# A two-layer metaformer block on one core: both expert layers with four experts per product, and a new order of work on every engine

## The chip, the core and the metric

The kernel runs on one core of a Trainium2 chip. The metric is the device time of one execution in microseconds (us), and the kernel is compared with itself by the median of several executions. The five engines each work through a list of instructions of their own, in order, and wait for one another on semaphores: TensorE (PE in the profile, with its weight loads as PEld), VectorE (DVE), ScalarE (ACT), GpSimd (POOL) and SyncE (SP, which here issues transfers and follows the control code). TensorE writes to PSUM, eight banks of 512 words in each of 128 partitions; the other three read PSUM or SBUF (GpSimd SBUF alone).

## What is computed

All data is 32-bit floating point. `x` holds 8 images of 32 channels and 24 x 24 points. Four sublayers follow one another, each added to its own input; each normalises first (subtract the mean over the channels, divide by the root of the variance).

```
x = x + conv0(ln_c(x))        # attention of every point to its 3x3 neighbours, 4 heads
t = t + experts(ln_t(t))      # 16 experts, each picks 8 of an image's 576 points
x = x + conv1(ln_c(x))        # products within 9x9 patches
t = t + chain(ln_t(t))        # up to 33 steps, chosen by argmax of one token
```

The second one is where most of the change lies:

```
logits = einsum('bsd,ed->bse', x, gate_w) + gate_b
probs  = softmax(logits, axis=1)                     # over the points
topv, topi = top 8 of probs for each image and expert
pooled = einsum('bked,bke->bed', x[topi], topv)      # 32 numbers per image and expert
h   = gelu(pooled @ weight1[e] + bias1[e])           # 128 hidden units
out = h @ weight2[e] + bias2[e]                      # back to 32
outputs[topi] += topv * out                          # scattered to the picked points
```

With the given data the chain at the end runs one step: a feed-forward layer on all points.

## The kernel before, in words

The images are worked on as two tiles, t = 0 and 1, of four images each: the 128 partitions are 4 images x 32 channels and the 576 points lie along a row, cut into two halves g = 0, 1 of 288. Banks 0 to 3 (`AB`) and 4 to 7 (`CD`) are shared out between the tiles. The order of work is written out by hand, one list per engine; the two tiles are woven into each other so that one tile's products cover the other's waits. Nothing is planned by a program.

A normalisation is `centre` (L451, a product with a centring matrix), squares on ScalarE (`squares`, L867), `variance` (L457, four products onto 32 partitions each), Ln and Exp on ScalarE (`inverse_std`, L881), `widen` (L468, spreads 1/std back over the channels), and `scale` on VectorE (L1049), which multiplies the widened factor in PSUM with the centred input kept in SBUF (`keep`, on ScalarE at L872 in `squares_keep`).

The attention: q, k, v products (L478); VectorE and GpSimd multiply q with nine shifted copies of k (L1067, L391); `head_sum` (L497) adds within a head; the maximum (L1192 to L1197), a subtraction (L1201), Exp (L957), a sum by TensorE into bank 7 (L691 to L694), Ln and Exp of it (L960, L962) and a multiplication (L1205) make the softmax. Then, for u = 0 to 5 (tile u // 3, row of neighbours u % 3), `spread(u)` (L518) gives the weights of a head to its channels: four products that read 32 partitions each, one for each quarter of the points, into banks 4 to 7; `terms(u)` on VectorE (L1074) multiplies the four quarters with v. `spread` waits for each quarter's bank by itself. GpSimd adds the terms up (`gsum`, L410; `x1_raw`, L420), and `add_centred` (L510) lets TensorE add and centre them at once, in banks 0 to 3, for the next normalisation.

The experts, for each tile: `gate` (L530) and the bias (`logits`, L888); `selection` on VectorE (L1086: eight largest, their replacement, and `pick`, L1095, which keeps the eight probabilities), Exp and the inverse sum on ScalarE (`probabilities`, L896); `turn_y`, `turn_pick` and `pooling` (L537, L547, L556) bring points onto partitions and pool the picked ones. `pooled` (L1102) masks the result so that each of the four images keeps its own 32 partitions. `hidden` (L569) is 16 products, one per expert, each with 128 x 128 weights and 4 columns; the weights of an expert lie four times on the partitions. Gelu follows, then `expert_out` (L580), 16 products with 128 x 32 weights and 4 columns, a turn (L588), `expert_blocks` on VectorE (L1110) and `scatter` (L591). For the third normalisation `keep_centred` (L564) first puts the centred input into the bank by two products with the identity, and the scatter adds the centred expert output on top. ScalarE loads another table of functions for Gelu and again for Ln and Exp; between `gelu(0)` and `gelu(1)` it does both (L974 to L981).

The patches (`pixels_out` L603 to `turn_back` L651) and the last normalisation are woven likewise; `choose` (L1147) finds the argmax of one token after the first third of `residual3(0, .)`. GpSimd builds a table of codes that `choose` reads (L401 to L408, on one partition of 627 words) behind its six q x k products. SyncE issues the constants in the order of L330 to L339; `x` of tile 1 and the first constants go through ScalarE's queue.

The lists themselves stand at L666 to L768 (TensorE), L933 to L1003 (ScalarE) and L1173 to L1246 (VectorE). The lines that matter most of them:

```
variance(1, 1); turn_pick(0); widen(1, 1)        # TensorE, L721 to L735
pooling(0); keep_centred(0); gate(1); hidden(0)
turn_y(1); turn_pick(1); expert_out(0)
pooling(1); keep_centred(1); scatter(0)
...
selection(0); turned_pick(0); scale(1, 1); pooled(0); selection(1)   # VectorE, L1213 to L1217
```

Of the kernel before, what the change touches and what calls it, by code (L numbers as in the profile page):

```python
# [9 lines left out]
P = 128  # L10
# [8 lines left out]
ER = E_ * TB  # L19
SC_, NCH = 96, S // 96  # L20
# [18 lines left out]
         ("wb", V2A), ("eb1", H1), ("eb2", C), ("pool", ER), ("own", TB), ("blk", GW), ("ebsel", ER), ("turn", 2 * C),  # L39
# [31 lines left out]
def pack_table(a):  # L71
# [24 lines left out]
    put("gb", np.repeat(a["L0_ffn_gate_b"], TB)[:, None])  # L96
# [7 lines left out]
    put("eb2", a["L0_ffn_weight2"][:, H1, :])  # L104
# [5 lines left out]
    put("turn", np.concatenate([np.eye(C), np.eye(C) - 1 / C], axis=1).astype(np.float32))  # L110
# [14 lines left out]
def expert_table(w):  # L125

    return np.tile(w[:, 0:C, :].transpose(1, 0, 2), (TB, 1, 1)).reshape(P, E_ * H1)
# [21 lines left out]
def metaformer(nc, x, L1_ffn_ffn_w1, L1_ffn_ffn_b1, L1_ffn_ffn_w2, L1_ffn_ffn_b2, L1_ffn_wq, L1_ffn_wk, L1_ffn_wv, L1_ffn_wo,  # L149
# [5 lines left out]
    with ctx:  # L155
# [19 lines left out]
        ew1 = sb("ew1", [P, E_, H1])  # L175
        ew2 = sb("ew2", [P, E_, C])
# [30 lines left out]
        pm = sb("pm", [P, T, ER])  # L207
        hidT = sb("hidT", [H1, T, ER])
        eoutT = sb("eoutT", [C, T, ER])
# [174 lines left out]
        def _(pool):  # L384
# [5 lines left out]

            for t in range(T):  # L391
# [8 lines left out]

            pool.wait_ge(mask_ld, 16 * 2)  # L401
            bits = code[:, :, :].rearrange("p b o -> p (b o)")
            nc.gpsimd.tensor_copy(maskf[:, :], mask_w[:, :]).then_inc(code_st, 1)
            pool.wait_ge(code_st, 1)
            nc.gpsimd.tensor_scalar(idle[:, :], maskf[:, :], 0.0, float(NONE), ALU.is_equal, ALU.mult).then_inc(code_st, 1)
            nc.gpsimd.tensor_tensor(maskf[:, :], maskf[:, :], rowc[:, :], ALU.add).then_inc(code_st, 1)
            pool.wait_ge(code_st, 3)
            nc.gpsimd.tensor_tensor(bits, maskf[:, :], idle[:, :], ALU.add).then_inc(code_st, 1)  # L408
# [35 lines left out]
        def _(pe):  # L444
# [73 lines left out]
            def spread(u):  # L518
# [235 lines left out]
            for k in range(4):  # L754
                gram_pair(1, k)
# [612 lines left out]
```

## Time and profile before

| | us |
|---|---|
| median of 3 executions | 164.44 |
| lowest and highest of them | 164.02, 165.64 |
| the profiled execution, whole | 165.66 |
| its span, first to last instruction | 163.8 |
| TensorE busy in the span | 136.1 (83%) |
| VectorE, ScalarE, GpSimd busy | 65.7, 48.2, 46.6 |
| mean clock granted to TensorE | 0.75 of full |

All times of the trace count from the start of the span. What lies around the span is 165.66 - 163.8 = 1.9 us. A product of 32-bit numbers shows as two records, so that "x32" of a line with 16 products is right. "Granted clock" is the share of TensorE's full clock (2.4 GHz) that it was given: 1.00, or 0.50, which is 1.2 GHz; a value in between is the mean over a stretch.

### The profile page before, as it was taken

The numbers are of one execution on the slowest core, as the hardware profiler recorded it, in microseconds if no ns is written. First come the engines' busy times: TensorE is split into PE (matmuls) and PEld (weight loads), VectorE is DVE, ScalarE is ACT, GpSimd is POOL, SyncE is SP. The second block draws the span as 40 slices with busy tenths as digits, with TensorE's granted clock in tenths as the row PEclk, the third lists the DMA queues.
The fourth block names the chain that finished last, engine by engine and source line by source line (L and its number), as shares of the span: only waits on it lengthen the run. The fifth ranks groups of instructions, "written<-read, shape, count | busy, mean of one in ns | idle before, by whom it ended". The sixth has DMA issues, their size and how long they took to land.

```text
span 163.8 us, 2345 instructions
## 1 busy us (share of the span) xinstructions
PE 136.1 (83%) x871; PEld 94.1 (57%) x871; DVE 65.7 (40%) x136; ACT 48.2 (29%) x116; POOL 46.6 (28%) x37
## 2 busy tenths in 40 slices
PE   0998986677996999999999945999998499677891
PEld 0455374543453576988769834596957367444630
DVE  0258939292555943713001004034711420406752
ACT  3334212300031390541060080305242064052522
POOL 8208995039159499900000000000000000303000
PEclk9999999975599999855555555569999555855558
DMA  5990000000000000000000000000000000010003
GB/s 174 386 262 2 4 0 0 4 0 0 0 0 0 2 2 4 0 0 4 0 0 0 0 0 0 0 4 0 0 0 4 0 0 0 0 20 4 2 0 144
DMA packets 3394, 4.18 MB, mean 26 GB/s; under 512 B 1974, under 2 KB 2614, under 8 KB 3256
## 3 DMA queue, kind: packets, MB, share of 16 engines
q1 hardware_dynamic: 3096, 3.54, 6.7%
q10 hardware_dynamic: 288, 0.51, 0.9%
q8 instruction: 7, 0.11, 0.3%
q14 instruction: 3, 0.02, 0.0%
HBM read 3.45 MB, written 0.59 MB: 25 GB/s over the span
## 4 chain that ended last, share of the span: by engine, by line
PE 72%; DVE 11%; ACT 6%; POOL 3%; issue 3%; DMA 2%; DVEq 1%; ACTq 0%
PE PS L574 7%; PE PS L513 6%; PE PS L637 5%; PE PS L480 5%; PE PS L474 4%; PE PS L647 4%; PE PS L613 4%; PE PS L454 3%; PE PS L526 3%; PE PS L596 3%; DVE prods L1082 3%; PE PS L623 3%; PE PS L561 3%; PE PS L464 2%; PE PS L600 2%
## 5 line engine op out<-in xcount | busy, mean ns | idle before, releaser
L440 POOL TENSOR_TENSOR y<-h,x 128x576 f32<-128x576 f32 x2 | 2.8, 1402 | 77.7 <-DVE h L1054 77.7
L870 ACT ACTIVATE sq<-PS 128x288 f32<-128x288 f32 x16 | 6.6, 411 | 36.6 <-PE PS L513 15.9
L1082 DVE TENSOR_TENSOR prods<-PS,vpad 128x432 f32<-128x432 f32 x24 | 13.0, 600 | 7.0 <-PE PS L526 6.8
L513 PE MATMUL PS<-prods,cst 128*128 128x288 f32 x36 | 12.2, 486 | 2.8 <-POOL prods L418 2.8
L415 POOL TENSOR_TENSOR prods<-prods 128x576 f32<-128x576 f32 x6 | 8.4, 1403 | 16.3 <-DVE prods L1082 16.3
L513 PEld LDWEIGHTS PS<-prods,cst 128*128 128x128 f32 x36 | 7.4, 219 | 8.4 <-POOL prods L418 4.4
L574 PE MATMUL PS<-pm,ew 128*128 128x4 f32 x64 | 11.5, 315 | 0.0
L574 PEld LDWEIGHTS PS<-pm,ew 128*128 128x128 f32 x64 | 11.3, 277 | 0.2
L526 PE MATMUL PS<-attn,wpk 32*128 32x432 f32 x48 | 9.3, 707 | 2.2 <-DVE attn L1205 1.4
L396 POOL TENSOR_TENSOR prods<-q_sb,kpad 128x576 f32<-128x576 f32 x6 | 7.7, 1337 | 7.8 <-ACT q_sb L947 7.8
L637 PE MATMUL PS<-U,xT 65*117 65x181 f32 x40 | 8.6, 368 | 0.0
L474 PE MATMUL PS<-rstd,cst 64*128 64x144 f32 x64 | 7.8, 374 | 0.8 <-ACT rstd L886 0.8
L480 PE MATMUL PS<-y,qkv_bd 128*128 128x288 f32 x24 | 7.4, 431 | 1.4 <-DVE y L1054 1.0
L1071 DVE TENSOR_TENSOR prods<-PS,kpad 128x576 f32<-128x576 f32 x12 | 8.1, 745 | 0.0
L884 ACT ACTIVATE lnv<-PS,cst 128x144 f32<-128x144 f32 x8 | 3.1, 383 | 16.5 <-PE PS L464 16.5
L825 PE MATMUL PS<-h,fw 32*128 32x384 f32 (+1 forms) x32 | 6.5, 730 | 1.7 <-issue 1.1
L474 PEld LDWEIGHTS PS<-rstd,cst 64*128 64x128 f32 x64 | 5.7, 236 | 3.7 <-ACT rstd L886 1.7
L1108 DVE COPY eoutT<-PS 32x64 f32<-32x64 f32 x2 | 0.4, 212 | 18.0 <-PE PS L584 18.0
L637 PEld LDWEIGHTS PS<-U,xT 65*117 65x117 f32 x40 | 7.0, 205 | 0.7 <-issue 0.6
L647 PE MATMUL PS<-gram,cval 117*64 117x117 f32 x40 | 7.1, 334 | 0.0
L647 PEld LDWEIGHTS PS<-gram,cval 117*64 117x64 f32 x40 | 5.6, 178 | 2.3 <-issue 1.9
L526 PEld LDWEIGHTS PS<-attn,wpk 32*128 32x128 f32 x48 | 3.7, 221 | 5.3 <-DVE attn L1205 3.1
(125 smaller groups left out, 239.3 us busy)
## 6 DMA issues: line engine op xcount, KB each, us to landing
ew<-in_experts SPq DMA_DIRECT2D x1, 1024.0 KB, 7.0
wpk<-in_pack SPq DMA_DIRECT2D x1, 705.0 KB, 5.6
result<-y SPq DMA_DIRECT2D x2, 288.0 KB, 2.2
U<-in_values SPq DMA_DIRECT2D x2, 162.5 KB
x_in<-in_x SPq DMA_DIRECT2D x2, 144.0 KB, 3.2
x_in<-in_x ACTq DMA_DIRECT2D x1, 288.0 KB, 3.8
ew<-in_experts SPq DMA_DIRECT2D x1, 256.0 KB, 8.0
cst<-in_first ACTq DMA_DIRECT2D x1, 209.0 KB, 3.1
```

The lines of the kernel that those rows point to most:

```text
L396: nc.gpsimd.tensor_tensor(prods[:, t, n, :].rearrange("p (r c) -> p r c", c=WW), q_sb[:, t, :].rearrange("p (r c) -> p r c", c=WW), kpad[: ...
L415: nc.gpsimd.tensor_tensor(total, a, prods[:, t, m * TRI + 1, :], ALU.add).then_inc(gsum_rdy[t], 1)
L474: last = nc.tensor.matmul(PS[:, AB[t][g], par * QS:(par + 1) * QS], sel[64 * g:64 * g + 64, par, :], rstd[64 * g:64 * g + 64, t, :], start ...
L480: nc.tensor.matmul(PS[:, bank, 0:HS], qkv_bd[:, w, :], cut(y, t)[:, g, :], start=True, stop=True).then_inc(signal, 1)
L513: done = nc.tensor.matmul(PS[:, AB[t][g], 0:HS], con("cen"), term[:, g * HS:(g + 1) * HS], start=first, stop=last, skip_group_check=True)
L526: nc.tensor.matmul(PS[:, 4 + q, 0:TRI * QS], heads[32 * q:32 * q + 32, t, :], attn[32 * q:32 * q + 32, m * TRI:(m + 1) * TRI, :].rearrange ...
L574: last = nc.tensor.matmul(PS[:, CD[t][0], e * TB:(e + 1) * TB], ew1[:, e, :], pm[:, t, e * TB:(e + 1) * TB], start=False, stop=True, skip_ ...
L637: last = nc.tensor.matmul(PS[0:GW, BK[t][GRAM_BANK[k]], i * (GW + V2):(i + 1) * (GW + V2)], xT[:, t, g * GW:(g + 1) * GW], U[:, t, g, :], ...
L647: last = nc.tensor.matmul(PS[0:V2, BK[t][YV_BANK[k]], i * GW:(i + 1) * GW], cval[:, t, 4 * k + i, :], gram[:, t, 4 * k + i, :], start=True ...
L870: nc.scalar.activation(cut(sq, t)[:, g, :], PS[:, AB[t][g], 0:HS], ACT.Square).then_inc(sq_rdy[t], 1)
L1071: nc.vector.tensor_tensor(prods[:, t, n, :].rearrange("p (g r c) -> p g r c", g=2, c=WW), rows24(both(AB[t])), k, ALU.mult).then_inc(prod_ ...
L1082: nc.vector.tensor_tensor(prods[:, t, m * TRI:(m + 1) * TRI, q * QS:(q + 1) * QS].rearrange("p n (r c) -> p n r c", c=WW), PS[:, 4 + q, 0: ...
```

## The change

The experts' weights are laid out otherwise: four experts share one product, each on its own 32 partitions (`EG` = 4, `NEG` = 4 products). To feed them, the pooled numbers of each image, now `pooled_j`, are copied to all four groups of partitions by one product (`replicate`, with the 128 x 128 table `same`), and VectorE masks them by expert (`mine`). The second layer's output stands on 128 partitions, masked by expert, and the turn adds the four groups. `keep_centred` goes; VectorE adds the scattered output to the kept centred input (`add_experts`), and the third normalisation squares it from SBUF. `gate`'s second half goes to partitions 64 to 127. `spread` waits for two quarters at a time, and can be called for one pair. The code table is built before the q x k products, its two transfers issued before those of `qkv` and `pack`. Two pairs of products whose results nobody reads (`keep_clock`) stand before and behind the softmax's sum. All lists of work are rearranged; copies of the centred input move from ScalarE to VectorE (`keep`) in the second tile of the second normalisation and in the last one.

```diff
+EG = P // C
+NEG = E_ // EG
...
+    put("same", (p[:, None] % C == p[None, :] % C).astype(np.float32))
+    put("mine", (p[:, None] // C == (er[None, :] // TB) % EG).astype(np.float32))
...
-    return np.tile(w[:, 0:C, :].transpose(1, 0, 2), (TB, 1, 1)).reshape(P, E_ * H1)
+    return w[:, 0:C, :].reshape(NEG, EG, C, H1).transpose(1, 2, 0, 3).reshape(P, NEG * H1)
...
+            sp.dma_start(mask_w[:, :], masks).then_inc(mask_ld, 16)
+            sp.dma_start(rowc[:, :], codes).then_inc(mask_ld, 16)
             sp.dma_start(qkv_bd[:, :, :].rearrange("p a b -> p (a b)"), qkv).then_inc(qkv_ld, 16)
             sp.dma_start(wpk[:, :], pack).then_inc(pack_ld, 16)
-            sp.dma_start(mask_w[:, :], masks).then_inc(mask_ld, 16)
-            sp.dma_start(rowc[:, :], codes).then_inc(mask_ld, 16)
...
+            def keep_clock(n, bank):
+                for i in range(n):
+                    nc.tensor.matmul(PS[:, bank, 0:HS], con("cen"), cut(x_in, 0)[:, 0, :], start=True, stop=True)
...
-                for q in range(4):
+                for pair in pairs:
                     if u >= 1:
-                        pe.wait_ge(term_rdy, 4 * (u - 1) + q + 1)
+                        pe.wait_ge(term_rdy, 4 * (u - 1) + 2 * pair + 2)
+                    for q in (2 * pair, 2 * pair + 1):
...
+            def replicate(t):
+                pe.wait_ge(pm_rdy[t], 1)
+                nc.tensor.matmul(PS[:, CD[t][1], ER:2 * ER], con("same"), pooled_j[:, t, :], start=True, stop=True).then_inc(pool_done[t], 1)
+                nc.tensor.matmul(PS[:, CD[t][0], 0:ER], con("eb1", E_), con("ebsel", E_), start=True, stop=False, skip_group_check=True)
+            def hidden(t):
+                pe.wait_ge(pm_rdy[t], 2)
+                for k in range(NEG):
...
+            keep_clock(2, VBANK)
             for n in range(NBR):
...
             last.then_inc(ssum_done, 1)
+            keep_clock(2, 4)
 
             spread(0)
             spread(1)
+            spread(2)
             pe.wait_ge(gsum_rdy[0], 2)
             add_centred(0, prods[:, 0, 0, :])
-            spread(2)
+            spread(3)
+            add_centred(0, prods[:, 0, 8, :])
+            spread(4, (0,))
             pe.wait_ge(gsum_rdy[0], 4)
             add_centred(0, prods[:, 0, 3, :])
-            spread(3)
-            add_centred(0, prods[:, 0, 8, :])
+            spread(4, (1,))
+            spread(5, (0,))
             pe.wait_ge(gsum_rdy[0], 5)
             add_centred(0, prods[:, 0, 6, :], last=True)
-            spread(4)
-            variance(1, 0)
+            spread(5, (1,))
             pe.wait_ge(gsum_rdy[1], 2)
             add_centred(1, prods[:, 1, 0, :])
-            widen(1, 0)
-            spread(5)
-            gate(0)
-            pe.wait_ge(gsum_rdy[1], 4)
-            add_centred(1, prods[:, 1, 3, :])
+            variance(1, 0)
             for g in range(2):
                 pe.wait_ge(term_rdy, 4 * 5 + 2 * g + 2)
                 for n in (6, 7, 8):
-                    add_centred(1, prods[:, 1, n, :], last=(n == 8), halves=(g,))
+                    add_centred(1, prods[:, 1, n, :], halves=(g,))
+            widen(1, 0)
+            pe.wait_ge(gsum_rdy[1], 4)
+            add_centred(1, prods[:, 1, 3, :], last=True)
+            gate(0)
             turn_y(0)
             variance(1, 1)
             turn_pick(0)
             widen(1, 1)
+            pooling(0)
+            gate(1)
+            replicate(0)
+            turn_y(1)
...
-            pooling(0)
-            keep_centred(0)
-            gate(1)
             hidden(0)
-            turn_y(1)
             turn_pick(1)
             expert_out(0)
             pooling(1)
-            keep_centred(1)
-            scatter(0)
+            expert_turn(0)
+            replicate(1)
+            scatter_centred(0)
             hidden(1)
+            scatter_raw(0)
+            expert_out(1)
             variance(2, 0)
-            expert_out(1)
+            expert_turn(1)
             widen(2, 0)
-            scatter(1)
+            scatter_centred(1)
+            scatter_raw(1)
             pixels_out(0)
...
-            turn_back(0)
             for k in range(4):
                 gram_pair(1, k)
+            turn_back(0)
+            values_of(1, 0)
             pe.wait_ge(x3_rdy[0], 1)
             token_of(xs[3])
+            gram_pair(1, 4)
             centre(3, 0)
-            values_of(1, 0)
-            gram_pair(1, 4)
+            values_of(1, 1)
             variance(3, 0)
-            values_of(1, 1)
+            values_of(1, 2)
             widen(3, 0)
-            values_of(1, 2)
             turn_back(1)
             centre(3, 1)
...
             gelu(0)
-            squares_keep(2, 0)
-            nc.scalar.preload_act_table_set("natural_log_exp_and_others")
-            inverse_std(2, 0)
-            nc.scalar.preload_act_table_set("gelu_and_others")
             gelu(1)
             nc.scalar.preload_act_table_set("natural_log_exp_and_others")
-            squares_keep(2, 1)
+            squares(2, 0, 0)
+            squares(2, 0, 1)
+            inverse_std(2, 0)
+            squares(2, 1, 0)
+            squares(2, 1, 1)
             inverse_std(2, 1)
...
+            def add_experts(t):
+                for g in range(2):
+                    dve.wait_ge(xc_done[t], 4 + g + 1)
+                    nc.vector.tensor_tensor(cut(xc, t)[:, g, :], PS[:, AB[t][g], 0:HS], cut(xc, t)[:, g, :], ALU.add).then_inc(xc_kept[t], 1)
...
+            terms(5)
             scale(1, 0)
-            terms(5)
+            keep(1, 1, 0)
+            keep(1, 1, 1)
             selection(0)
+            scale(1, 1)
             turned_pick(0)
-            scale(1, 1)
-            pooled(0)
+            pooled_images(0)
             selection(1)
+            pooled_experts(0)
+            turned_pick(1)
             expert_rows(0)
-            turned_pick(1)
+            pooled_images(1)
             expert_blocks(0)
-            pooled(1)
+            pooled_experts(1)
+            add_experts(0)
...
             dve.wait_ge(code_st, 4)
+            for k in range(4):
+                gram_mask(1, k)
             residual3(0, 0)
             choose(0, 0)
             residual3(0, 1)
             residual3(0, 2)
-            for k in range(4):
-                gram_mask(1, k)
             gram_mask(1, 4)
+            keep(3, 0, 0)
+            keep(3, 0, 1)
             scale(3, 0)
```

## Rows read from the trace of the kernel before

**Rows 1.** The page, span in 40 slices: TensorE's granted clock in tenths.

```profile
PEclk9999999975599999855555555569999555855558
```

**Rows 2.** Windows of 2 us: busy us (count) of PE, PEld, DVE, ACT, POOL; clock; DMA.

```profile
34.00:36.00 2.00, 1.87 (x7) 1.71 (x8) 2.00 (x4) 0.00 (x0) 0.40 (x1) 0.65 0.00 0
...
44.00:46.00 2.00, 2.00 (x11) 0.64 (x10) 0.97 (x3) 0.00 (x0) 1.17 (x1) 0.79 0.00 0
...
68.00:70.00 2.00, 2.00 (x14) 2.00 (x14) 1.87 (x1) 0.79 (x4) 1.43 (x2) 0.68 0.00 0
...
84.00:86.00 2.00, 2.00 (x5) 0.95 (x4) 0.00 (x0) 1.95 (x3) 0.00 (x0) 0.50 0.00 0
```

**Rows 3.** Chain of work, the softmax: start us, us, what.

```profile
25.87 1.21 DVE smax L1197
...
28.46 2.46 PE PS L693 x18
...
32.28 1.09 PE PS L526 x8
```

**Rows 4.** Timeline of GpSimd, products and code table.

```profile
13.05 7.72 POOL L396 TENSOR_TENSOR prods<-q_sb,kpad 128x576 f32<-128x576 f32 x6 [7.82 <-ACT q_sb L947]
...
25.39 1.51 POOL L408 TENSOR_TENSOR code<-h,x 1x627 f32<-1x627 f32 x1
```

**Rows 5.** Chain of work, spreads, terms and sums.

```profile
42.58 2.22 PE PS L513 x4
44.80 1.00 PE PS L526 x8
45.81 2.14 DVE prods L1082 x4
...
53.84 1.11 PE PS L534 x4
54.95 4.08 PE PS L513 x16
```

**Rows 6.** Timeline of TensorE: start, us, instruction, idle us before it and what ended it.

```profile
24.86 2.21 PE L513 MATMUL PS<-x_in,cst 128*128 128x288 f32 x8
...
96.82 1.87 PE L584 MATMUL PS<-hidT,ew 128*32 128x4 f32 x32 [2.39 <-ACT hidT L915]
...
102.25 2.28 PE L596 MATMUL PS<-pick,ebd 64*128 64x288 f32 x4 [1.52 <-DVE ebd L1117]
...
130.71 2.29 PE L454 MATMUL PS<-x,cst 128*128 128x288 f32 x4 [2.24 <-DVE x L1143]
```

**Rows 7.** Chain of work, the experts.

```profile
60.07 1.16 PE PS L552 x12
...
63.49 1.03 PE PS L567 x4
...
65.99 4.39 PE PS L574 x32
...
72.18 2.11 PE PS L552 x12
74.29 1.82 PE PS L584 x32
...
79.75 2.03 PE PS L567 x4
...
86.53 6.92 PE PS L574 x32
...
106.45 3.73 PE PS L613 x18
```

**Rows 8.** Chain of work, the last normalisation.

```profile
132.99 1.75 PE PS L647 x8
134.74 1.49 PE PS L637 x4
...
142.88 0.77 PE PS L454 x2
```

More of the change, by code:

```diff
@@ L38 @@
 _PACK = [("hsum", 2 * 32), ("heads", 2 * P), ("idn", P), ("gate", ER), ("conv", CP), ("gb", 1), ("bconv", CP), ("wa", V2A),
-         ("wb", V2A), ("eb1", H1), ("eb2", C), ("pool", ER), ("own", TB), ("blk", GW), ("ebsel", ER), ("turn", 2 * C),
+         ("wb", V2A), ("eb1", H1), ("eb2", P), ("pool", ER), ("same", P), ("mine", ER), ("own", TB), ("blk", GW), ("ebsel", ER),
+         ("turn", 2 * C),
          ("istep", NB_), ("one", 1)]
@@ L95, in pack_table @@
     put("conv", conv)
-    put("gb", np.repeat(a["L0_ffn_gate_b"], TB)[:, None])
+    put("gb", np.tile(np.repeat(a["L0_ffn_gate_b"], TB), 2)[:, None])
     bias = np.zeros((V2, CP), np.float32)
@@ L103, in pack_table @@
     put("eb1", a["L0_ffn_weight1"][:, C, :])
-    put("eb2", a["L0_ffn_weight2"][:, H1, :])
+    put("eb2", np.tile(a["L0_ffn_weight2"][:, H1, :], (1, EG)))
+    put("same", (p[:, None] % C == p[None, :] % C).astype(np.float32))
+    put("mine", (p[:, None] // C == (er[None, :] // TB) % EG).astype(np.float32))
     put("pool", (p[:, None] // C == er[None, :] % TB).astype(np.float32))
@@ L109, in pack_table @@
     put("ebsel", (e[:, None] == er[None, :] // TB).astype(np.float32))
-    put("turn", np.concatenate([np.eye(C), np.eye(C) - 1 / C], axis=1).astype(np.float32))
+    put("turn", np.tile(np.concatenate([np.eye(C), np.eye(C) - 1 / C], axis=1), (EG, 1)).astype(np.float32))
     put("istep", STEP * np.arange(NB_, dtype=np.float32)[None, :])
@@ L389, in _ @@
             pool.wait_ge(ones_set, 1)
+            pool.wait_ge(mask_ld, 16 * 2)
+            bits = code[:, :, :].rearrange("p b o -> p (b o)")
+            nc.gpsimd.tensor_copy(maskf[:, :], mask_w[:, :]).then_inc(code_st, 1)
+            pool.wait_ge(code_st, 1)
+            nc.gpsimd.tensor_scalar(idle[:, :], maskf[:, :], 0.0, float(NONE), ALU.is_equal, ALU.mult).then_inc(code_st, 1)
+            nc.gpsimd.tensor_tensor(maskf[:, :], maskf[:, :], rowc[:, :], ALU.add).then_inc(code_st, 1)
+            pool.wait_ge(code_st, 3)
+            nc.gpsimd.tensor_tensor(bits, maskf[:, :], idle[:, :], ALU.add).then_inc(code_st, 1)
+            pool.wait_ge(code_st, 4)
             for t in range(T):
@@ L516, in add_centred, with spread @@
                         done.then_inc(xc_done[t], 1)
-            def spread(u):
+            def spread(u, pairs=(0, 1)):
                 t, m = divmod(u, TRI)
@@ L867, in squares @@
             def squares(i, t, g):
[L869 to L870 removed]
+                if i == 2:
+                    act.wait_ge(xc_kept[t], 2 * i + g + 1)
+                    src = cut(xc, t)[:, g, :]
+                else:
+                    act.wait_ge(xc_done[t], 2 * i + g + 1)
+                    src = PS[:, AB[t][g], 0:HS]
+                nc.scalar.activation(cut(sq, t)[:, g, :], src, ACT.Square).then_inc(sq_rdy[t], 1)
             def keep(t, g):
@@ L965, in _ @@
             inverse_std(1, 0)
+            squares(1, 1, 0)
+            squares(1, 1, 1)
             logits(0)
             probabilities(0)
-            squares_keep(1, 1)
+            inverse_std(1, 1)
             turned_y(0)
-            inverse_std(1, 1)
             logits(1)
@@ L989, in _ @@
             cval_copy(0, 4)
+            yv_copy(0, 1)
             for k in range(NP):
                 u_copy(1, k)
-            for k in (1, 2):
-                yv_copy(0, k)
+            yv_copy(0, 2)
             for k in range(4):
                 cval_copy(1, k)
-            squares_keep(3, 0)
             yv_copy(1, 0)
+            squares(3, 0, 0)
+            squares(3, 0, 1)
             cval_copy(1, 4)
+            yv_copy(1, 1)
             inverse_std(3, 0)
-            for k in (1, 2):
-                yv_copy(1, k)
-            squares_keep(3, 1)
+            yv_copy(1, 2)
+            squares(3, 1, 0)
+            squares(3, 1, 1)
             inverse_std(3, 1)
```

87 lines of the change are left out of this document (41 added, 46 removed).

## The prediction

> **What bounds the kernel now.** I read the page's slices first, then windows of 2 us, then the chain of waits, then the timelines of the engines. The chain gives TensorE 72% of the span, so the question at each place is what TensorE does there and at which clock. The slices show two long low stretches [rows 1]. Windows date them [rows 2]: the mean of 0.65 in 34 to 36 puts the first fall at 34.6, the 0.79 of 44 to 46 the return at 44.8, the 0.68 of 68 to 70 the next fall at 68.7; by the slices that stretch ends near 109. Ahead of the first fall TensorE waited much of its time for VectorE; ahead of the second it ran products of 4 columns each. So three things cost: the first expert layer, whose time is weight loads; the low clock that lies over the experts; and waits between engines.
>
> **Early part.** `smax` (L1197, 128 x 144) takes 1.21 us from 25.87 [rows 3] and so ends at 27.08, just behind GpSimd's L408, at 25.39 + 1.51 = 26.90 [rows 4]. I read that as a wait for GpSimd; its own time is then about 0.3 (a `terms` of 432 columns takes 2.14 / 4 = 0.54 [rows 5]; a third of it and a fixed part). The Trainium skill ("SBUF — State Buffer", section "Who interferes with whom") has this as a rule: a VectorE operation with two SBUF inputs contends with a GpSimd one that reads SBUF, and the later one waits. The trace agrees with it; were it otherwise, `smax` would stay as long as it is, and the gain of this part would be nothing.
> With the table built earlier, 0.9 goes here. The first `keep_clock` takes most of it back: TensorE ends its sums of x at 24.86 + 2.21 = 27.07 [rows 6], two products of 288 columns are four records of 4.08 / 16 = 0.26 [rows 5], so the softmax's sum starts at 28.15 in place of 28.46 [rows 3]: gain 0.3, and `spread(0)` starts at 32.0 in place of 32.28. The second pair takes 1.05 in the wait between that sum's end (28.15 + 2.46 = 30.6) and 32.0, and costs nothing; without that cover, 1.05.
> The build itself: GpSimd idles from 13.05 - 7.82 = 5.23 to 13.05; the build now follows the products, from 20.77 to 26.90, 6.1 long [rows 4], so it would end at 11.4 and fit. The landing of its two small transfers isn't shown; for a delay of the products between nothing and 1 us, I take nothing. Moved ahead, they put two issues in front of `qkv` and `pack` on SyncE; the chain holds no transfer but the first constants, so no work waits for either, and of the expert tables behind them one shrinks to a quarter. Nothing.
>
> **Spreads and sums.** The first three spreads are paced by VectorE, 2.14 a set [rows 5]; a pair takes up to a set's 1.0, under the 1.08 of two terms, so `spread(2)` ends near 38.5. From there TensorE waits little, since each of GpSimd's sums is asked for a set later. Left up to the end of `gate(0)`: nine sums of four records, 1.05 each, 9.45; four calls of spread at 1.0 (a lone pair costs as much as a set), 4.0; the gate 1.11 [rows 5]; variance and widen, eight short records each, put at another 1.1; handovers 0.45. That is 16.1, so at full clock `gate(0)` ends at 54.6. Before, it ended at 54.95 [rows 5], with tile 1's sums behind it, to 59.03; now these are done.
> The clock decides what holds of that. The low activity that brought it down at 34.6 is still there from 32 to 38; the dummies fill only what lies ahead of it. I expect the fall at 36 to 38 and the return near 44, because from 38.5 on sums and spreads stand back to back, as they did ahead of the return at 44.8. From 38.5 to 44 TensorE is the limit at half speed (a sum takes 2.22 [rows 5]): 5.6 / 2 = 2.8 lost; `gate(0)` ends at 57.4. Behind it stands the chain of logits, maximum, Exp and pick: 5.1 before (54.95 to 60.07 [rows 5, 7]), in which VectorE still had `terms(5)`; I take 4.0. `turn_pick(0)` starts at 61.4 against 60.07: **+1.3**.
> A rule speaks against this order: the Trainium skill ("TensorEngine Tiling (Array Packing)", section "Key Properties") says that a change of the tiling mode drains TensorE, and spreads (32 rows) and sums (128 rows) alternate three times more often now. By that rule something is due for each. The rows leave little room: a spread between sums takes 1.00 [rows 5], the first one, behind a wait, 1.09 [rows 3]. Between 0 and 0.3, with three changes of 0.1, I take the upper end, **+0.3**.
>
> **Experts, `turn_pick(0)` to `pixels_out(0)`.** 46.4 before (60.07 to 106.45 [rows 7]).
> Removed: `keep_centred`, 1.03 + 2.03 = 3.1 [rows 7]. The first layer: 32 records took 4.39 and, at low clock, 6.92, which is 0.216 each [rows 7]; eight a tile now, all at low clock, 2 x 8 x 0.216 = 3.5: 7.8 less (16 columns to stream for 4 should hide in the weight load). The second layer: 1.82 for 32 records with 32 weight columns [rows 7], 1.7 for eight with 128: 0.2 in both tiles. Waits: Gelu(1) behind a table load, 2.39, and `ebd`, 1.52 [rows 6], with 0.3 at the turn: 4.2, since Gelu(1) needs no load now and other products stand in front of the others.
> Added: two copies of 64 columns at 0.6 and wider biases at 0.3 a tile, 1.8, between 1.2 and 2.4. Two waits: `turned_pick(0)` now stands behind `scale(1, 1)` on VectorE, which waits for widen, and pooling(0) for both: 1.1. `pooled_experts(0)` stands behind `selection(1)` and its Exp, and hidden(0) waits for it; gate(1), the copy and `turn_y(1)` cover all but 0.85, up to 3 if that cover is gone. `add_experts`, about 0.5 a half on VectorE, lies beside hidden(1), and the squares are needed only behind `expert_out(1)`: nothing; uncovered, 1 a tile.
> Clock: with tile 1's sums gone from there, TensorE idles some 2.5 between `gate(0)` and `turn_pick(0)` and has little on both sides. I expect the fall at 60 to 64 in place of 68.7. `turn_pick`, widen and pooling, 3.4 at full clock (60.07 to 63.49), then take 2.11 / 1.16 as long [rows 7], +2.8, and a bias +0.3. `gate(1)` I leave at its length, since its halves go to separate partitions now and may overlap; else +1.
> Sum: -3.1 - 7.8 - 0.2 - 4.2 + 1.8 + 1.95 + 3.1 = -8.45, taken as **-8.5**, between -5 and -11.
>
> **Patches and the last normalisation.** Before, TensorE waited 2.24 for `choose` and `residual3` ahead of `centre(3, 0)` [rows 6], and only then did `values_of(1, 0)` and `gram_pair(1, 4)`, 1.75 + 1.49 = 3.2 [rows 8]. Now these stand ahead, in that wait: -3.2; if the wait gets longer by them, nothing. The token comes a little earlier, and copies leave ScalarE for VectorE: -0.7 for both, by estimate. `centre(3, 1)`, at 142.88 before [rows 8], met a high clock (slice 35 of rows 1), and perhaps doesn't now: +0.3. Together **-3.6**, between -1 and -5. The weights of the last step are fetched behind `residual3(1)`, which moves along. The step itself is as before.
>
> **Sum.** +1.3 + 0.3 - 8.5 - 3.6 = -10.5 (the early 0.3 is in the 32.0). The profiled execution took 165.66 (span 163.8 and 1.9 around it), so one like it takes 155.2. It lies 1.2 above the median of 164.44, from which I count: **153.9**.
>
> **Rivals.**
> A: the dummies hold the clock through the terms. For: they fill the two waits ahead of the fall. Against: from 32 to 38 VectorE's pace leaves TensorE idle a good part of the time. It gains the 2.8: 151.1.
> B: the experts' new waits aren't covered, 1.5 more a tile: 157. For: pooled, copy, mask and product go back and forth between TensorE and VectorE, with `selection(1)` ahead of a mask. Against: gate, turns and scatter stand between.
> C: the clock is back only with tile 1's sums. The work from 38.5 to 48 takes twice as long, 9.6 more, and 2 till it returns, in place of 2.8: +8.8, 162.7. For: a pair reads half the partitions, and in 84 to 86 TensorE is busy throughout, with products that read 64 partitions, and stays at 0.50 [rows 2]. Against: each pair is followed by a sum over all 128.
> D, the other side: as C, but the clock stays low through `gate(0)` and on to the patches. 16.1 more in place of 2.8: +13.3, 167.2. Slower by over 1% it gets only if some 15 are lost, nearly the whole stage at half. Against: tile 1's six half sums in a row.
> E: the change doesn't do what it says in the first layer, because its eight records wait for one another instead of streaming: at twice 0.216 each, 3.5 of the 7.8 are lost, 157.4.
>
> **How the numbers follow.** Forecast 0.53, A 0.20, B 0.10, C 0.08, D 0.04, E 0.05. A measurement of this kernel tells about 1%, so 162.8 to 166.1 is no change. Forecast, A, B, E and a little of C are faster, 0.91; the rest of C, 0.05, is within; D, 0.04, is slower. The range runs from A with the better end of the experts' sum, 149.5, to the middle between B and C, 160.0.
>
> **What would show it.** Right: `smax` near 0.3; sums and spreads without gaps from 38.5 on, and a low stretch there under 10 us; eight records a tile in the first layer, near 0.22 each; no wait of 2.4 ahead of the second; the low clock before 65; `values_of(1, 0)` ahead of `centre(3, 0)`. Wrong: TensorE idle over 1 us ahead of the copy or of hidden; first-layer records above 0.4; a low stretch over 12 us in the terms; a wait for `choose` as long as before with the two products in front of it.

## The result and the profile after

The changed kernel takes 154.72 us (median of four executions, 154.63 to 155.16). The kernel before took 164.23 beside it; the ratio is 0.9414 (95% interval 0.9351 to 0.9477), so it is 5.9% faster. Forecast was 153.9, between 149.5 and 160.0. The medians fell by 9.5; the profiled execution fell from 165.66 to 155.16 (span 153.3), by 10.5, as the prediction's sum had it. That agreement is partly luck: four of the five stretches below were off by 0.7 to 0.85, two each way, and these errors cancel. (Executions over 1.5% above the fastest of their kernel are left out of the ratios; where that matters, single times are given.)

| stretch | before | after | change | predicted |
|---|---|---|---|---|
| start to `spread(0)` | 32.28 | 32.15 | -0.13 | -0.3 |
| `spread(0)` to `turn_pick(0)` | 27.79 | 30.37 | +2.58 | +1.9 |
| `turn_pick(0)` to `pixels_out(0)` | 46.38 | 38.66 | -7.72 | -8.5 |
| `pixels_out(0)` to `centre(3, 1)` | 36.43 | 32.05 | -4.38 | -3.6 |
| `centre(3, 1)` to the end | 20.92 | 20.07 | -0.85 | 0 |

The predicted column is the prediction's working cut at the same points: 61.7 - 32.0 less 27.79 is +1.9, for example.

Clock by slices, for [rows 1]:

```profile
PEclk9999999996559999655555555559999965995567
```

Windows of the kernel after, for [rows 2] (columns as there):

```profile
34.00:36.00 2.00, 1.49 (x6) 0.83 (x8) 1.88 (x4) 0.00 (x0) 0.53 (x1) 0.84 0.00 0
44.00:46.00 2.00, 2.00 (x8) 1.18 (x4) 1.74 (x4) 0.00 (x0) 0.00 (x0) 0.60 0.00 0
62.00:64.00 2.00, 1.48 (x10) 1.51 (x11) 0.37 (x1) 1.73 (x5) 1.92 (x2) 0.66 0.02 4
102.00:104.00 2.00, 2.00 (x13) 2.00 (x12) 0.73 (x3) 0.00 (x0) 0.00 (x0) 0.60 0.00 0
```

A mean of 0.84 is 32% of the window at half clock, so the first fall is at 35.4; 0.60 puts the return at 45.6: 10.2 us low, as long as before. The next low stretch begins at 62.7 (0.66) and ends at 103.6 (0.60). It sets in six us earlier than before, just behind TensorE's wait of 2.08 ahead of the experts' first step, and lies over all of both expert layers.

VectorE's timeline, for [rows 3], and GpSimd's, for [rows 4]:

```profile
26.40 0.31 DVE L1245 TENSOR_TENSOR smax<-smax 128x144 f32<-128x144 f32 x1
```

```profile
9.98 1.50 POOL L404 TENSOR_TENSOR code<-h,x 1x627 f32<-1x627 f32 x1
13.57 7.71 POOL L413 TENSOR_TENSOR prods<-q_sb,kpad 128x576 f32<-128x576 f32 x6 [2.08 <-ACT q_sb L983]
```

`smax` went from 1.21 to 0.31. The code table ends at 11.48 and GpSimd then waits 2.08 for q: the products aren't delayed by it.

Chain of work, for [rows 3, 5]:

```profile
28.57 2.22 PE PS L717 x18
...
32.15 1.09 PE PS L541 x8
...
34.51 5.76 PE PS L541 x16
40.27 2.22 PE PS L527 x4
...
57.83 0.69 PE PS L549 x4
```

L717 is the softmax's sum, L541 `spread`, L527 the sums, L549 `gate(0)`, which ends at 58.52. Two sets of spreads take 5.76, mostly at half clock and partly waiting.

TensorE's timeline of the experts, for [rows 6, 7]:

```profile
62.52 2.04 PE L567 MATMUL PS<-diag,pick 64*96 64x64 f32 x12 [2.08 <-DVE pick L1134]
...
67.16 2.79 PE L576 MATMUL PS<-pickT,yT 96*128 96x64 f32 x12 [1.48 <-DVE pickT L1139]
...
75.16 1.86 PE L590 MATMUL PS<-pooled_e,ew 128*128 128x16 f32 x8 [1.37 <-DVE pooled_e L1147]
...
79.67 1.89 PE L601 MATMUL PS<-hidT,ew 128*128 128x16 f32 x8
...
87.99 1.89 PE L590 MATMUL PS<-pooled_e,ew 128*128 128x16 f32 x8
```

L590 is the first layer: eight records take 1.86, 0.23 each, against 4.39 and 6.92 for 32. L601, the second layer, has no idle time in front of it where Gelu(1) cost 2.39. New are three waits for VectorE: 2.08, 1.48 and 1.37.

The same timeline, the last normalisation, for [rows 6, 8]:

```profile
122.19 0.19 PE L686 MATMUL PS<-wpk,x 32*1 32x32 f32 x1
122.31 0.87 PE L660 MATMUL PS<-U,xT 65*117 65x181 f32 x4
124.61 2.29 PE L468 MATMUL PS<-x,cst 128*128 128x288 f32 x4 [1.43 <-DVE x L1191]
...
133.23 1.24 PE L468 MATMUL PS<-x,cst 128*128 128x288 f32 x4 [1.39 <-DVE x L1191]
135.06 0.45 PE L478 MATMUL PS<-sq,cst 128*32 128x144 f32 x8 [0.60 <-DVE xc L1086]
136.36 0.77 PE L488 MATMUL PS<-rstd,cst 64*128 64x144 f32 x8 [0.84 <-ACT rstd L922]
138.84 1.66 PE L856 MATMUL PS<-h,fw 32*128 32x384 f32 x8 [1.71 <-issue]
```

`gram_pair(1, 4)` (L660) now stands between the token's product (L686) and `centre(3, 0)`, whose wait is 1.43 in place of 2.24. Before, the token's product was the last ahead of that wait:

```profile
128.26 0.21 PE L663 MATMUL PS<-wpk,x 32*1 32x32 f32 x1
```

Variance and widen behind `centre(3, 1)` ran at full clock here (0.45, 0.77).

### The profile page after: what moved, and what is told of

Same layout as the page of the kernel before. It is cut to its first block, busy times and chain, and to the rows that moved or that the text cites. A ratio compares the mean times of both kernels' runs of the same rounds, so it can differ in the third digit from the quotient of the medians.

```text
span 153.3 us, 2162 instructions
## 1 busy us (share of the span) xinstructions
PE 129.2 (84%) x779; PEld 86.5 (56%) x779; DVE 68.0 (44%) x148; ACT 43.5 (28%) x104; POOL 46.7 (30%) x37
## 4 chain that ended last, share of the span: by engine, by line
PE 78%; DVE 8%; ACT 6%; issue 4%; DMA 2%; DVEq 1%; ACTq 0%
PE PS L527 9%; PE PS L541 7%; PE PS L494 5%; PE PS L468 5%; PE PS L488 4%; PE PS L856 4%; PE PS L660 4%; PE PS L670 4%; PE PS L636 4%; PE PS L576 4%; PE PS L646 3%; PE PS L567 3%; PE PS L623 3%; PE PS L616 3%; PE PS L518 3%
## 5 line engine op out<-in xcount | busy, mean ns | idle before, releaser
L906 ACT ACTIVATE sq<-PS 128x288 f32<-128x288 f32 x12 | 4.9, 412 | 32.8 <-PE PS L527 22.2
L541 PE MATMUL PS<-attn,wpk 32*128 32x432 f32 x48 | 11.7, 751 | 1.8 <-DVE prods L1121 1.4
L527 PE MATMUL PS<-prods,cst 128*128 128x288 f32 x36 | 12.3, 480 | 0.0
L527 PEld LDWEIGHTS PS<-prods,cst 128*128 128x128 f32 x36 | 7.3, 219 | 6.2 <-issue 3.3
L1086 DVE COPY xc<-PS 128x288 f32<-128x288 f32 x10 | 4.6, 457 | 11.8 <-ACT sq L906 11.8
L541 PEld LDWEIGHTS PS<-attn,wpk 32*128 32x128 f32 x48 | 3.7, 235 | 7.4 <-issue 4.0
L468 PE MATMUL PS<-x_in,cst 128*128 128x288 f32 x8 | 4.0, 619 | 4.0 <-DMA cst<-in_first 4.0
L660 PE MATMUL PS<-U,xT 65*117 65x181 f32 x40 | 7.1, 324 | 0.1
L1093 DVE TENSOR_TENSOR y<-PS,xc 128x288 f32<-128x288 f32 x8 | 3.3, 451 | 8.6 <-PE PS L488 8.6
L576 PE MATMUL PS<-pickT,yT 96*128 96x64 f32 x24 | 5.6, 423 | 1.5 <-DVE pickT L1139 1.5
L1185 DVE TENSOR_TENSOR gram<-PS,wpk 117x234 f32<-117x234 f32 x10 | 3.9, 398 | 6.3 <-PE PS L660 6.2
L670 PE MATMUL PS<-gram,cval 117*64 117x117 f32 x40 | 6.5, 311 | 0.0
L660 PEld LDWEIGHTS PS<-U,xT 65*117 65x117 f32 x40 | 6.0, 180 | 0.7 <-issue 0.6
```

Of the source, the lines that this page charges most:

```text
L468: nc.tensor.matmul(PS[:, AB[t][g], 0:HS], con("cen"), cut(src, t)[:, g, :], start=True, stop=True).then_inc(xc_done[t], 1)
L527: done = nc.tensor.matmul(PS[:, AB[t][g], 0:HS], con("cen"), term[:, g * HS:(g + 1) * HS], start=first, stop=last, skip_group_check=True)
L541: nc.tensor.matmul(PS[:, 4 + q, 0:TRI * QS], heads[32 * q:32 * q + 32, t, :], attn[32 * q:32 * q + 32, m * TRI:(m + 1) * TRI, :].rearrange ...
L576: last = nc.tensor.matmul(PS[:, CD[t][1], 0:ER], yT[:, t, c, :], pickT[:, t, c, :], start=(c == 0), stop=(c == NCH - 1))
L660: last = nc.tensor.matmul(PS[0:GW, BK[t][GRAM_BANK[k]], i * (GW + V2):(i + 1) * (GW + V2)], xT[:, t, g * GW:(g + 1) * GW], U[:, t, g, :], ...
L670: last = nc.tensor.matmul(PS[0:V2, BK[t][YV_BANK[k]], i * GW:(i + 1) * GW], cval[:, t, 4 * k + i, :], gram[:, t, 4 * k + i, :], start=True ...
```

## The experiments

Theory: weight loads, waits and the place of the last products make the gain, and the low clock gives some of it back; what holds the clock is TensorE being kept busy in its waits. Rivals stand with each run. Times are medians, ratios are to the kernel before; "after" is the changed kernel, 154.72. Results of the products called dummies are read by nobody.

**The dummies out.**

```diff
-            keep_clock(2, VBANK)
...
-            keep_clock(2, 4)
```

> The changed kernel (154.7 us) without its four products that nobody reads. My theory: they bring the fall of the clock in the terms about 1 us later and no more, and cost 0.5 us ahead of the softmax's sum, which starts at 28.57 behind them, though Exp's first part is done at 27.95. So 154 to 155.5, with smax unchanged at 0.3, the sum ending near 30.3 in place of 30.79, and the fall of the clock before 35.4. Rival: the dummies are what keeps the terms' low stretch from being longer; then it grows by 2 to 4 us and the time goes to 156 or 157.

Measured: 155.00, ratio 0.9389 (0.9324 to 0.9455): no difference from after's 0.9414. Windows of this kernel:

```profile
36.00:38.00 2.00, 1.67 (x7) 0.70 (x8) 1.97 (x4) 0.00 (x0) 1.92 (x2) 0.86 0.00 0
44.00:46.00 2.00, 2.00 (x11) 1.06 (x8) 1.97 (x4) 0.00 (x0) 0.00 (x0) 0.94 0.00 0
```

The low stretch runs from 37.4 to 44.2, 6.8 us against 10.2 with the dummies; the fall was expected before 35.4. The four dummies of the change neither prevent it nor make it shorter.

**The code table late again.**

```diff
+            sp.dma_start(qkv_bd[:, :, :].rearrange("p a b -> p (a b)"), qkv).then_inc(qkv_ld, 16)
+            sp.dma_start(wpk[:, :], pack).then_inc(pack_ld, 16)
             sp.dma_start(mask_w[:, :], masks).then_inc(mask_ld, 16)
             sp.dma_start(rowc[:, :], codes).then_inc(mask_ld, 16)
-            sp.dma_start(qkv_bd[:, :, :].rearrange("p a b -> p (a b)"), qkv).then_inc(qkv_ld, 16)
-            sp.dma_start(wpk[:, :], pack).then_inc(pack_ld, 16)
...
```

(and the table's five operations back behind the q x k products)

> The changed kernel with the code table built behind the q x k products again and its two transfers issued behind those of qkv and pack. My theory: smax goes from 0.31 back to about 1.2 us, because it meets GpSimd's last operation on the table, but the dummies hid half of that: the softmax's sum starts at about 28.9 in place of 28.57 and ends 0.4 later; 155.1. Rival 1: the early table is worth its whole 0.9, 155.6. Rival 2: smax was slow for another reason and stays at 0.3; 154.7.

Measured: 156.06, ratio 0.9453 (0.9396 to 0.9510); the interval overlaps that of after, so the size isn't settled. The place is. VectorE's and GpSimd's timelines:

```profile
26.67 1.22 DVE L1245 TENSOR_TENSOR smax<-smax 128x144 f32<-128x144 f32 x1
```

```profile
26.17 1.54 POOL L416 TENSOR_TENSOR code<-h,x 1x627 f32<-1x627 f32 x1
```

`smax` takes 1.22 again and ends at 27.89, just behind GpSimd's 27.71. The softmax's sum then starts 2.51 behind the start of `smax` (29.18 on the chain), against 2.17 in after: 0.34 later, as expected.

**Twelve dummies in TensorE's waits ahead of the experts.** 

```diff
             variance(1, 1)
+            keep_clock(4, 7)
             turn_pick(0)
             widen(1, 1)
+            keep_clock(3, 7)
             pooling(0)
...
+            keep_clock(5, 7)
             hidden(0)
```

> The changed kernel with twelve more products that nobody reads, in three places where TensorE waits in the experts: 4 ahead of turn_pick(0), 3 ahead of pooling(0), 5 ahead of hidden(0). My theory: the clock falls at 62.7 because tile 1's sums no longer fill the wait ahead of turn_pick(0); with the dummies it stays at full till behind hidden(0), and turn_pick 2.0, widen 1.1, pooling 2.8, gate 1.2 and the copy 1.2 take about half: 2 to 4 us less, 151 to 153. Rival: TensorE's sparse work lets the clock fall anyway; the dummies then run at half clock, 1.0 us each, and push the work behind them: 156 to 160.

Measured: 148.91, ratio 0.9033 (0.8962 to 0.9103), 5.8 under after. TensorE's timeline:

```profile
62.08 1.20 PE L567 MATMUL PS<-diag,pick 64*96 64x64 f32 x12
...
65.36 1.51 PE L576 MATMUL PS<-pickT,yT 96*128 96x64 f32 x12
...
68.88 2.59 PE L461 MATMUL PS<-x_in,cst 128*128 128x288 f32 x10
71.47 1.06 PE L590 MATMUL PS<-pooled_e,ew 128*128 128x16 f32 x8
...
74.90 1.95 PE L576 MATMUL PS<-pickT,yT 96*128 96x64 f32 x12
```

The three waits are filled (L461 is the dummy) and the clock falls at 75.8 in place of 62.7. What the low clock had cost: turn_pick 2.04 to 1.20, pooling 2.79 to 1.51, the first layer 1.86 to 1.06; in TensorE's timelines `turn_pick(0)` to `pixels_out(0)` takes 31.7 in place of 38.6. The theory holds and was too small. But the window of the fall shows its limit:

```profile
74.00:76.00 2.00, 2.00 (x19) 2.00 (x18) 0.78 (x2) 0.00 (x0) 0.00 (x0) 0.96 0.04 8
```

TensorE had no idle time there, with turn_pick(1), expert_out(0) and pooling(1) back to back, and the clock fell all the same. Filled waits alone don't hold it; what about these products lets it fall, no run here separates.

**The old order of the last part.**

```diff
+            turn_back(0)
             for k in range(4):
                 gram_pair(1, k)
-            turn_back(0)
-            values_of(1, 0)
             pe.wait_ge(x3_rdy[0], 1)
             token_of(xs[3])
+            centre(3, 0)
+            values_of(1, 0)
             gram_pair(1, 4)
-            centre(3, 0)
+            variance(3, 0)
             values_of(1, 1)
-            variance(3, 0)
+            widen(3, 0)
             values_of(1, 2)
-            widen(3, 0)
...
```

(and the copies and masks that go with it, on ScalarE and VectorE)

> The changed kernel with the order of the kernel before from the second tile's gram products on, on TensorE, ScalarE and VectorE (the copies of the centred input stay on VectorE). My theory: values_of(1, 0) and gram_pair(1, 4) return behind centre(3, 0), at low clock 3.2 us, and TensorE waits over 2 us for choose again; with the later turn_back 3 to 4.5 us are lost, 158 to 159. Rival: the clock did it, since the last widen and variance ran at full clock in the changed kernel; then only 1 to 2 are lost, 156 to 156.5.

Measured: 159.42, ratio 0.9672 (0.9584 to 0.9761): 4.7 above after (4.2 by the ratios). TensorE's timeline:

```profile
124.80 1.24 PE L468 MATMUL PS<-x,cst 128*128 128x288 f32 x4 [2.24 <-DVE x L1191]
125.97 1.82 PE L670 MATMUL PS<-gram,cval 117*64 117x117 f32 x8
127.72 1.56 PE L660 MATMUL PS<-U,xT 65*117 65x181 f32 x4
```

Wait and products are back as in [rows 6, 8]. Not all of the loss is theirs. In the profiled pair `pixels_out(0)` to `centre(3, 1)` is 3.0 longer (35.13 against 32.12), of which 0.75 lies in `pixels_out` itself (4.16 against 3.41), ahead of all that was reordered, where the low clock lasts longer; and from `centre(3, 1)` on 1.2 more is lost (21.26 against 20.07), with variance and widen at half clock again. So the rival, the clock, has some 2 of these 4.2, by estimate from these numbers.

**Four experts per product, and nothing else of the change, on the kernel before.** (Its edit is the lines of the diff on `EG`, `NEG`, `replicate` and the masks.)

> The kernel before (164.4 us) with one part of the change: four experts per product in both layers, with the copy and the two masks that feed them, and nothing else moved. My theory: of the prediction's terms this has the first layer's -7.8, the second's -0.2, the copies' and biases' +1.8 and nothing of the rest; the copies stand where other products run, so no wait is added: -6, 158 to 159.5. Rival: the way from the pooled numbers over copy and mask to the first layer is longer by two handovers a tile, and eats half of it: 161 to 162.

Measured: 156.10, 157.95, 159.43 and 159.57, median 158.69; ratio of the lower two 0.9530 (0.9406 to 0.9654). By that ratio the grouping alone makes 7.7 of the 9.5 us, by its interval 5.7 to 9.8. TensorE's timeline, of the execution of 159.57:

```profile
66.88 1.06 PE L585 MATMUL PS<-pooled_e,ew 128*128 128x16 f32 x8
...
90.64 1.89 PE L596 MATMUL PS<-hidT,ew 128*128 128x16 f32 x8 [2.39 <-ACT hidT L929]
```

The first layer takes 1.06 here, at full clock, and 1.89 in tile 1 (85.10); in the full change it is 1.86 and 1.89. The wait for Gelu(1) stays, so the other lists remove that. "No wait is added" was wrong: TensorE now waits 1.93 for `pick` ahead of turn_pick(1), at 71.03.

**The identity products back.**

```diff
+            keep_centred(0)
             scatter_centred(0)
...
+            keep_centred(1)
             scatter_centred(1)
```

(`scatter_centred` adds onto them; VectorE copies the sum in place of adding)

> The changed kernel (154.7 us) with keep_centred again: two products with the identity ahead of each tile's scatter, which adds onto them; VectorE copies the sum in place of adding. My theory: at low clock these are 2.2 us a tile, on the path for both, so 4 to 4.5 more, 158.5 to 159. Rival: one tile's pair lies in a wait of TensorE (for ebd or the table load), and only 2 are lost, 156.5.

Measured: 155.29, 155.45, 155.49, and 160.28, 160.58; ratio of the lower three 0.943 (0.9325 to 0.9534). These three don't differ from after's 0.9414, so theory and rival both miss. Their mean clock is 0.797, above after's 0.771 to 0.788; the other two have 0.773 and 0.759. Only the execution of 160.58 was profiled, so whether the higher clock hides the time of the products in the three isn't shown: inconclusive. I repeated it on a steadier kernel.

**Dummies also in the last normalisation, on the kernel with the twelve.**

```diff
+            keep_clock(3, 0)
             centre(3, 0)
...
+            keep_clock(2, 5)
             centre(3, 1)
+            keep_clock(1, 5)
             variance(3, 1)
+            keep_clock(2, 5)
             widen(3, 1)
+            keep_clock(4, 5)
```

> The kernel gap_dummies (148.9 us) with twelve more products that nobody reads in TensorE's waits of the last normalisation: 3 ahead of centre(3, 0), 2 ahead of centre(3, 1), 1 and 2 around variance(3, 1), 4 behind widen(3, 1). My theory: the stretch from 117 us on and the last layer then run at full clock: centre, values, variance and widen 2 to 3 us less, the last layer's products 6.4 and 3.1 at half clock shrink to what ScalarE and VectorE need, 2 to 3 less: 143.5 to 145. Rival: the last layer is bound by the relus and the clock there is worth nothing, 146 to 147; or the dummies come in the way of centre, 149.

Measured: 146.68, ratio 0.8908 (0.8831 to 0.8985), executions within 146.0 and 147.0. 2.2 less, within the rival's 146 to 147: from 97 on the clock stays up until 133, by its slices, but the gain lies ahead of the last step. `pixels_out(0)` to `centre(3, 1)` takes 29.8 in place of 32.2, and from there to the end it takes 20.3, against 20.1 with the twelve alone. That the clock was up for the last layer's first products, from 130 to 133, bought nothing.

**The identity products on that kernel.** (The edit of `keep_centred` above.)

> The kernel with dummies in the gap and in the last normalisation (146.68), with the two identity products a tile back and VectorE copying in place of adding; its executions lie closer together than those of the changed kernel. Theory of the prediction: the identity products are 3.1 on the path, as before; at the low clock that holds there each tile's four records take 2.29, so 148.8 to 151. Rival: they stand in waits for VectorE, and part of their time is covered: 146.9 to 148.

Measured: 151.13, ratio 0.9190 (0.9121 to 0.9260): 4.45 above 146.68. TensorE's timeline:

```profile
78.46 2.29 PE L615 MATMUL PS<-xc,wpk 128*128 128x288 f32 x4
...
92.19 2.29 PE L615 MATMUL PS<-xc,wpk 128*128 128x288 f32 x4
```

Two times 2.2 at low clock account for the difference, just over the theory's 151: in this kernel the identity products stand wholly on the path, and the rival falls. That they cost as much in the changed kernel isn't shown.

**Dummies between the steps of the experts, on the kernel with the twelve.**

```diff
             hidden(0)
+            keep_clock(1, 0)
             turn_pick(1)
+            keep_clock(1, 0)
             expert_out(0)
+            keep_clock(1, 0)
             pooling(1)
+            keep_clock(1, 0)
...
             hidden(1)
+            keep_clock(2, 2)
             scatter_raw(0)
             expert_out(1)
+            keep_clock(1, 2)
             variance(2, 0)
             expert_turn(1)
+            keep_clock(1, 2)
             widen(2, 0)
```

> The kernel gap_dummies (148.9 us) with eight more products that nobody reads, between the experts' steps behind hidden(0). My theory: in gap_dummies the clock falls at 75.9 and returns at 96.2; at full clock this stretch's products take about half, so from 20.3 us some 10 go, and the eight dummies cost 0.55 each on the path, 4.4, and some waits of the other engines show: 3 to 5 less, 144 to 146. Rival: the eight are too few, the clock falls a little later, and they cost what they gain: 148 to 150.

Measured: 141.37, 150.22, 156.68 and 157.00; no ratio, and neither theory nor rival covers them. Mean clocks are 0.923, 0.860, 0.831 and 0.818. The best is 7.5 under the kernel with the twelve. Only the execution of 150.22 was profiled; its clock falls behind hidden(1), at 82.7:

```profile
82.00:84.00 2.00, 2.00 (x7) 1.07 (x7) 0.00 (x0) 1.97 (x4) 0.00 (x0) 0.68 0.00 0
```

There `turn_pick(0)` to `pixels_out(0)` takes 34.2, against 31.7 with the twelve alone: where the clock falls among them, the dummies cost 2.6. Where the two longest lose their time isn't shown.

**Dummies also in the terms, on the kernel with those in the last normalisation.**

```diff
             spread(0)
+            hold_clock(3)
             spread(1)
+            hold_clock(1)
             spread(2)
```

(`hold_clock` is the same product on 224 columns, into a free part of bank 1; the text below says 288)

> The kernel with dummies in the gap ahead of the experts and in the last normalisation (146.68), and four more products of 288 columns: three behind spread(0), one behind spread(1). Theory: TensorE waits there for VectorE's terms, and the low stretch from about 35 to 46 costs the 2.8 that the prediction gave it; the four cost nothing, and the time is 143.7 to 144.5. Rival: from 38 to 46 VectorE and GpSimd set the pace, so that a full clock there buys nothing: 146.2 to 147.2. Second rival: the clock falls all the same, and four products, some 2 us, stand on the path: 147.5 to 149.

Measured: 142.30, ratio 0.8646 (0.8581 to 0.8711): 4.4 under 146.68. The low stretch of the terms is gone, and both rivals with it; the theory was too small. `spread(0)` to `turn_pick(0)` takes 26.6 in place of 30.5, which is 3.8 of the 4.4. The page:

```profile
PEclk9999999999999999999995555559999999999777
```

**All of them.** (The edits of `hold_terms_end` and `hold_experts` together.)

> The same with eight more products between the steps of the two expert layers. Theory: the clock falls at 75 because the products there have few columns; filled, it stays up through the experts, and the time is 139 to 142 with a mean clock above 0.90. Rival: as in the kernel with dummies in the experts and not in the terms, it falls anyway in some executions, where the eight then take twice as long: single executions from 140 up to 155, the median above 146.

Measured: 137.84 (136.53 to 138.14), ratio 0.8365 (0.8297 to 0.8434): 16.9 under after, from 36 products whose results are never used. It beats both kernels. Its page, then its chain through the terms, then two lines of TensorE's timeline:

```profile
PEclk9999999999999999999999999999999999999559
```

```profile
32.82 1.01 PE PS L546 x8
33.83 1.33 PE PS L466 x6
...
35.19 1.93 PE PS L546 x8
37.12 0.58 PE PS L466 x2
37.69 1.69 PE PS L546 x8
39.38 1.17 PE PS L532 x4
...
54.76 0.69 PE PS L554 x4
```

```profile
68.85 1.06 PE L595 MATMUL PS<-pooled_e,ew 128*128 128x16 f32 x8
...
78.08 1.06 PE L595 MATMUL PS<-pooled_e,ew 128*128 128x16 f32 x8
```

The mean clock is 0.975. Both first layers run at full clock. The theory's reason for the fall at 75, few columns, isn't tested by this. Only four executions were timed, and the same eight dummies without those in the terms and in the last normalisation spread over 16 us: how safely the clock holds is open.

**Spread waiting for each quarter again.**

```diff
                     if u >= 1:
-                        pe.wait_ge(term_rdy, 4 * (u - 1) + 2 * pair + 2)
+                        pe.wait_ge(term_rdy, 4 * (u - 1) + 2 * pair + 1)
                     for q in (2 * pair, 2 * pair + 1):
+                        if u >= 1 and q % 2 == 1:
+                            pe.wait_ge(term_rdy, 4 * (u - 1) + q + 1)
```

> The changed kernel (154.72, ratio 0.9414), with spread waiting for each quarter's bank by itself again, all else as changed. Theory: the third spread starts one term (0.6) earlier but ends with the same last quarter, so the sums behind it start when they did: 154.3 to 155.2. Rival: two quarters at a time is what lets sums and spreads stand back to back, and single waits stop TensorE between them: 156 to 157.5. Second rival: each earlier quarter lets VectorE start earlier, 0.5 a set over three sets: 153 to 153.5.

Measured: 154.41, ratio 0.9420 (0.9355 to 0.9484): the same as after. Waiting in pairs is worth nothing by itself.

## Why the prediction was right, point by point

**Early part: right.** `smax` 0.31 for "about 0.3", and 1.22 with the table late. The Trainium skill ("SBUF — State Buffer", "Who interferes with whom") has a VectorE operation with two SBUF inputs contend with a GpSimd one that reads SBUF; both traces agree. The first pair of dummies takes about half of the gain, not most of it: the softmax's sum started 2.59 behind the start of `smax` before (28.46 - 25.87), starts 2.17 behind it in the changed kernel (28.57 - 26.40) and 1.69 without dummies (28.85 - 27.16). (The prediction's 27.07 and four records of 0.26 make 28.11, not 28.15; nothing hangs on it.)

**Terms: mechanism right, lag mis-sized (+0.7).** The kernel with all dummies shows the stage at full clock: `spread(2)` ends 6.56 after the start of `spread(0)` (39.38 - 32.82; predicted 38.5 - 32.0 = 6.5), and `gate(0)` ends 16.07 later (55.45; predicted 16.1). The changed kernel took 8.12 and 18.25. So the lag is 1.56 + 2.18 = 3.74, not 2.8: the step that failed said that VectorE paces the spreads up to 38.5 whatever the clock. With the clock down from 35.4, the second and third set took 5.76, waits included, and ended at 40.27. I also put the return "near 44"; it came at 45.6, and the low stretch of 10.2 is just over the 10 that I had named as a sign of being right. The 0.3 for changes of tiling rested on a miscount: the work changes between spreads and other products nine times in the list before and nine times in the list after, so nothing more was due. The Trainium skill ("TensorEngine Tiling (Array Packing)", "Key Properties") has a change of the tiling mode drain TensorE. No cost of that shows: the stage took 16.07 at full clock where 16.1 were summed without it. The 4.0 from `gate(0)` to `turn_pick(0)` is 4.00 (58.52 to 62.52). No run undoes the new order of the terms by itself.

**Experts: -7.7 for -8.5.** The first layer: 3.7 for 3.5 (1.86 + 1.82 on the chain). `keep_centred`: 3.1 in the old trace; wholly on the path, and 4.4 at low clock, in `end_centred`; in the changed kernel itself its worth is open. The fall at 62.7 lies in "60 to 64". Mis-sized are the new waits: 1.1 and 0.85 predicted, 1.48 and 1.37 measured, 0.9 more. That is a part of rival B, in one tile only; by the prediction's own test (TensorE idle over 1 us ahead of hidden) its cover of 0.85 was wrong.

**Patches and last normalisation: -4.4 for -3.6.** The old order costs 4.2 when put back, some 2 of it by the clock. I had both products go into the wait of 2.24. Only `gram_pair(1, 4)` did, and the wait fell to 1.43 by its 0.87: from the token's product to `centre(3, 0)` it takes 2.42, against 2.45 before. `values_of(1, 0)` stands ahead of the token's product, which comes 0.8 earlier after `pixels_out(0)` all the same (122.19 - 101.11 against 128.26 - 106.38 in TensorE's timelines); from it to `centre(3, 1)` the time fell from 14.62 to 11.04. The +0.3 for `centre(3, 1)` was not due: its first half takes 0.77 on both chains.

**The last step: -0.85 for 0.** "As before" failed. From `centre(3, 1)` to the end of widen the time fell from 4.84 to 3.90, because the clock came back sooner (variance 0.97 to 0.45, widen 1.34 to 0.77); TensorE's wait behind widen grew from 1.10 to 1.71, and the rest of the step is 0.5 shorter. The sum did not price where the clock changes in this part.

**Rivals.** A fell as a claim on four dummies in the wrong place; as a price it was too low (2.8 for what is 3.7, and 4.4 with what follows). C and D fell: the clock came back at 45.6, ahead of tile 1's sums. E fell: 0.23 a record. The range's lower end is a slip: A's 151.1 with the better end of the experts' sum, 2.5 less, is 148.6 and not 149.5.

## What to carry to other kernels

When the granted clock falls, look at where TensorE waited just before, and put products that nobody reads into those waits. Here those that fitted a wait cost nothing (`turn_pick(0)` starts 4.78 behind the start of `gate(0)` with four of them and 4.76 without), and the gain is what then runs at full clock. Look again at where the clock falls next, since a busy TensorE alone didn't hold it at 75.8, and time several executions: where the clock falls among the fillers, they are added work at half speed. Price a stage from both levels, each step's records at low clock too, and not only those steps that TensorE is seen to pace at full clock.

## What I had not expected

The size: the whole change gave 9.5, and 36 unread products, some 18 us of TensorE's own time (about 0.5 each on the chain), gave another 16.9. The four that the change puts around the softmax give nothing; with four more in the waits that follow, from 33 to 38, the clock stayed up through the terms.

The same kernel's executions can differ by 16 us (141.37 to 157.00) with the same work, and the mean clock goes with it. With the clock up throughout, executions lie within 1.6.

At the start, the clock is recorded as full but the first products take as long as at half clock, or longer: the chain of the changed kernel has, for four records of one line,

```profile
3.98 2.59 PE PS L468 x4
6.57 1.19 PE PS L478 x8
7.76 1.33 PE PS L468 x4
```

2.59 and 1.33 in slices that the page marks 9; four such records took 2.29 at half clock (at 124.61). What the first products wait for, no run here tells.
